# A graph kernel's first edge stretch: own rows in runs of four per partition

## The reference

```
src, dst = edges + one self loop per node
xl = x @ Wl ; xr = x @ Wr
logits = einsum(leaky_relu(xl[src] + xr[dst]), att)      # per edge and head
alpha  = softmax of the logits over the edges of one dst
out    = segment_sum(alpha * xl[src], dst) + bias        # then graph norm, elu, skip, layer norm
# twice: h = tanh(segment_sum(sum_b c[etype,b] * h[src] @ basis[b]) + h @ loop_w + bias)
```

## Time and profile before

| what | us |
|---|---|
| median of 3 runs | 3410.07 |
| lowest, highest | 3409.99, 3412.36 |
| profiled execution: its span, the only time the profile gives for it | 4033.8 |
| PE busy in the span | 3226.5 (80%) |
| POOL busy | 2055.6 (51%) |
| DVE busy | 2357.5 (58%) |
| ACT busy | 1828.3 (45%) |

### The profile page before, as it was taken

The page is one execution under the profiler, slowest core; times in us unless marked ns, Lnnn a source line. Parts: engine busy times, 40 slices in busy tenths (PEclk is TensorE's granted clock), DMA queues, the critical chain, the costliest instruction groups (busy, mean ns, idle before and its releaser), DMA issues.

```text
span 4033.8 us, 65767 instructions
## 1 busy us (share of the span) xinstructions
PE 3226.5 (80%) x17551; PEld 2290.4 (57%) x17551; DVE 2357.5 (58%) x7747; ACT 1828.3 (45%) x4347; POOL 2055.6 (51%) x2407
## 2 busy tenths in 40 slices
PE   3778777778778758888987888887996888886887
PEld 2666656666556545557874444445884444444665
DVE  3444344444444348897875666664444666665998
ACT  1333333334334324447993444443443444444665
POOL 5555555555555502225766666661226666662555
PEclk8988888889899879999998999998998988998999
DMA  3333333334333338877972333335993333333998
GB/s 82 97 101 95 93 93 92 94 95 105 92 94 102 86 78 239 241 230 252 291 253 81 88 84 83 83 83 167 299 299 88 84 82 81 84 85 117 341 326 279
DMA packets 660630, 579.29 MB, mean 144 GB/s; under 512 B 74468, under 2 KB 535173, under 8 KB 660261
## 3 DMA queue, kind: packets, MB, share of 16 engines
q1 hardware_dynamic: 494580, 335.02, 28.5%
q0 software_dynamic: 67008, 156.44, 14.3%
q10 hardware_dynamic: 98672, 83.61, 6.3%
HBM read 366.34 MB, written 208.43 MB: 142 GB/s over the span
## 4 chain that ended last, share of the span: by engine, by line
PE 36%; issue 16%; another core or an unknown queue 13%; ACT 12%; DVE 11%; DMA 4%; ACTq 3%; SPq 2%; POOL 1%; DVEq 0%; POOLq 0%
PE bank L1073 15%; PE bank L1084 4%; ACT work L1317 3%; PE bank L1120 3%; PE bank L1127 2%; DMA work<-w_d 2%; PE bank L1064 2%; DMA w_d<-work 1%; DVE work L1927 1%; ACTq L430 1%; ACT work L1309 1%; PE bank L1140 1%; PE bank L1094 1%; DVE work L1813 1%
## 5 line engine op out<-in xcount | busy, mean ns | idle before, releaser
L1927 DVE SCALAR_TENSOR_TENSOR work<-bank,coef,work 128x128 f32<-128x128 f32 x2400 | 664.5, 343 | 490.2 <-ACT work L1351 269.3
L1073 PE MATMUL bank<-basis_s,work 128*128 128x512 f32 x1600 | 815.9, 634 | 39.4 <-issue 18.1
L785 POOL DMA_INDIRECT work<-in_x_dram,slot_src x400 | 386.0, 965 | 497.5 <-PE bank L887 345.5
L827 POOL DMA_INDIRECT work<-h_d,slot_src x400 | 393.9, 985 | 230.2 <-issue 104.9
L827 POOL DMA_INDIRECT work<-x_d,slot_src x400 | 393.3, 983 | 226.9 <-issue 107.2
L785 POOL DMA_INDIRECT work<-in_x_dram,slot_dst x400 | 386.4, 966 | 123.6 <-issue 123.6
L1073 PEld LDWEIGHTS bank<-basis_s,work 128*128 128x128 f32 x1600 | 293.8, 205 | 272.9 <-issue 242.5
L1650 DVE TENSOR_TENSOR work<-work,bank 128x512 f32<-128x512 f32 x100 | 68.8, 688 | 608.5 <-ACT bank L1200 531.2
L1351 ACT ACTIVATE work<-bank,coef 128x128 f32<-128x128 f32 x800 | 288.4, 365 | 293.5 <-PE bank L1073 147.0
L1084 PEld LDWEIGHTS bank<-work 128*126 128x126 f32 x1600 | 217.9, 203 | 290.2 <-issue 228.3
L1084 PE MATMUL bank<-work 128*126 128x128 f32 x1600 | 233.3, 293 | 171.7 <-ACT work L1357 95.4
(11 more groups left out here) (278 smaller groups left out, 7547.7 us busy)
## 6 DMA issues: line engine op xcount, KB each, us to landing
w_d<-work SPq DMA_DIRECT2D x800, 62.5 KB
work<-in_x_dram SPq DMA_DIRECT2D x194, 256.0 KB, 4.5
work<-x_d SPq DMA_DIRECT2D x194, 256.0 KB, 4.4
w_d<-work SPq DMA_DIRECT2D x400, 66.9 KB
work<-w_d SPq DMA_DIRECT2D x398, 64.0 KB, 3.4
work<-w_d ACTq DMA_DIRECT2D x390, 64.0 KB, 3.4
xl_d<-work SPq DMA_DIRECT2D x97, 256.0 KB
work<-xl_d SPq DMA_DIRECT2D x97, 256.0 KB, 3.8
```

The lines of the kernel that those rows point to most:

```text
L785: pool.indirect_dma_start(quad(k, i % 3)[:, c, :], None, x, bass.IndirectOffsetOnAxis(ap=table[:, a:a + 1], axis=0)).then_inc(e_in[i % 3], 16)
L827: pool.indirect_dma_start(quad(0, i % 3)[:, c, :], None, (x1_d, h1_d)[l], bass.IndirectOffsetOnAxis(ap=slot_src[:, a:a + 1], axis=0)).then ...
L1073: pe.matmul(psum[YBANKS[k % 5]][:, :], quad(1, i % 2)[:, c, :], basis_s[:, l, :, :].rearrange("k b n -> k (b n)"), start=True, stop=True). ...
L1927: ins = dve.scalar_tensor_tensor(o, psum[YBANKS[k % 5]][:, b * D:(b + 1) * D], coef[:, i, l, c, b:b + 1], o, ALU.mult, ALU.add)
```

## The change

Loads and stores of the own rows go through `run_rows`. After the transposes, column t * 128 + p of bank A is then node 4p + t of the quad. ACT's copy writes it to column 4p + t, so that the copy in SBUF is in node order, as before; it now writes every element 16 bytes from the one before. The matmul for the self logits reads its stationary operand as before. The one for xl must leave node 4p + t in partition p of tile t, so that the store can go out in runs; its stationary operand is every fourth column, again 16 bytes apart. The last quad stays as it was.

```diff
             def load_own(q):
-                for to, part in node_quad(x, q, quad(9, q % 3), True):
+                for to, part in run_rows(x, q, quad(9, q % 3), True):
             def save_xl(q):
-                for to, part in node_quad(xl_d, q, quad(11, q % 3), False):
+                for to, part in run_rows(xl_d, q, quad(11, q % 3), False):
             def project_own(q):
+                runs = work[10][:, q % 2 * 512:(q % 2 + 1) * 512].rearrange("d (p t) -> d t p", t=4)
                 for t in range(4):
                     at = slice(t * P, (t + 1) * P)
-                    pe.matmul(LEFT[:, at], quad(10, q % 2)[:, t, :], w_lr[:, 0:D], start=True, stop=True)
+                    own = runs[:, t, :] if q < QUADS - 1 else quad(10, q % 2)[:, t, :]
+                    pe.matmul(LEFT[:, at], own, w_lr[:, 0:D], start=True, stop=True)
             def own_turned(q):
-                act.activation(flat(10, q % 2), A[:, :], ACT.Copy).then_inc(qt_cp, 1)
+                to, turned = quad(10, q % 2, P), A[:, :].rearrange("d (t p) -> d t p", t=4)
+                if q < QUADS - 1:
+                    to = flat(10, q % 2).rearrange("d (p t) -> d t p", t=4)
+                act.activation(to, turned, ACT.Copy).then_inc(qt_cp, 1)
```

## The result

The changed kernel takes 3455.36 us (median of 4 runs, 3454.96 to 3457.93) against 3410.03 us for the kernel before in the same session (3407.58 to 3412.36): 1.4% slower, ratio 1.0139 with a 95% interval of 1.0125 to 1.0153. The forecast was no change.

A forecast was written before the change was run, and what follows sets the result against it. The prediction took POOL's gathers to bound all three edge stretches, 10.0 us a row in the first, with PE close behind. Every term was 0 on the path, so 3410.07 + 0 = 3410 us, range 3385 to 3460.

The forecast's parts named there:

- weights of the xl matmul: Line 916, strided weight loads on PE: 0 to 0.88 us a row, taken as 0, covered by the matmul before.
- rival A: Line 916: strided weights make PE the bound, slower, 3422 to 3495 us, centre 3440; chance 0.24.
- POOL's pace as the bound before: First edge stretch: unprofiled, POOL's gathers set 10.0 us a row, inferred from 619.3 of 623.7 us profiled excess.
- The sign of being wrong at the prediction's end: Time moving over 7 us with POOL's spacing unchanged would mean the first stretch was not at POOL's rate.
- PE's need: First edge stretch: PE busy 9.68 of each 10.0 us row at full clock, 0.32 us to spare.
- The copy on ACT: Line 1184, strided write: 0 to 0.61 us more a row, covered, so value 0; without cover 59 us.
- Rival C: ACT's copy runs late and shows on PE's 926 and DVE's 1650: 3420 to 3439 us; chance 0.07.
- The transfers: Own rows' loads and stores in 2 KB pieces: 0.2 to 0.6 us less DMA time a row, off the path, 0.
- the trace disagrees: Against the DMA page's line rate from 512 bytes: 512 bytes took 28 ns, 2 KB 76 to 100.
- Rival B: Fewer pieces shorten late waits behind the two transfers, faster: 3352 to 3400 us, centre 3385; chance 0.26.

The follow-up runs named there:

- all_weights: The changed kernel with the self logits' matmul weights strided too, 16 strided loads a row in place of 8: 3555.0 us, ratio 1.041.
- weights_only: The kernel before with only the xl matmul's weights read at a 16-byte stride, for 97 quads: 3455.66 us, ratio 1.0118.
- half_weights: The changed kernel with only two of the four tiles' weights strided, four strided loads a row: 3408.71 us, ratio 0.9989.
- seven_before: The kernel before without the fourth chain's gather of destination rows from row 3 on, seven gathers a row: 3364.0 us, ratio 0.9848.
- runs_only: The kernel before with only the loads and stores of the own rows in runs of four: 3412.75 us, ratio 0.9989.
- before_again: The kernel before, unchanged, profiled a second time: ratio 1.0001, profiled span 3419.3 us.

## Why the prediction was wrong

**What failed.** The term "weights of the xl matmul": I took 0, the lower bound, on the ground that the load is covered by the matmul before it. It is not. PE spends 0.22 us on a float32 matmul without a stride and 0.465 with it; per load that is 0.12 us more, nearly all of the 320 - 191 = 129 ns by which the record grew. The price is 0.97 us a row from the timeline (0.95 between after and all_weights), above the upper bound of 0.88, and rival A's mechanism is what happened, by weights_only, all_weights and half_weights. The prediction's own words were a warning: a load is covered if it "stays under 0.11 us", and the record that it read took 208 ns. How much of a record is the engine's own time the trace of before does not tell.

**POOL's pace as the bound before: right, size off.** The inference from the excess of the first profile held in the main: in the second profile POOL waits for nobody, and the second stretch runs at 1.27 us a gather. That the sum closed to 4 us (619 of 624) was partly luck: the first stretch runs at 10.28 us a row, not 10.0, since some gathers take longer than their 944 ns median. So PE's room was 10.28 - 9.74 = 0.54 us a row, not 0.32. The sign of being wrong at the prediction's end misled too: the time moved by 45 us with the gathers as they were, and yet the first stretch had been at POOL's rate. What changed is that PE took over.

**PE's need: right in size, by luck.** 9.68 us a row was read, 9.74 measured with seven gathers. But 9.68 is the busy time of one row with pauses in it, and that row has no `weigh` (lines 960 and 965 do not run in it); rows with `weigh` need more. Where PE sets the pace, in seven_before, line 897 starts each row, and two rows without `weigh` lie between these:

```profile
509.93 1.13 PE L897 MATMUL bank<-work,w_lr 128*128 128x512 f32 x2
...
528.54 1.13 PE L897 MATMUL bank<-work,w_lr 128*128 128x512 f32 x2
```

That is 9.3 us for each, and 10.16 and 9.74 us for the rows with `weigh` around them (starts at 499.77 and 538.28). With the true numbers the sum closes: eight strided loads in 97 of the 99 intervals are 0.97 x 97 / 99 = 0.95 us, PE needs 9.74 + 0.95 = 10.69 us, POOL 10.28, so 0.41 us x 99 = 41 us of the stretch; measured 41.1 in the profiles, and 45 us (3455.36 - 3410.03) in the runs.

**The copy on ACT: right on cover, and the price was within the bounds.** 1107 to 1110 ns for 616 is +0.49 us a row (I had 0 to 0.61), with no effect alone (0.9999) or beside a second copy (1.0001). Rival C falls.

**The transfers: 0 on the path, right; their price, wrong.** The path is shown by runs_only. In all 660,629 - 586,133 = 74,496 packets are gone (74,500 foretold), but not the engines' time: the prediction had 0.2 to 0.6 us a row to gain, and runs_only shows none (28.1% and 28.4%). Its 100 ns a packet on q1 was a mean with small packets in it, about 1,500 of the 13,824 with four bytes; those of 2 KB alone took 112 ns there as well. Only on q10, in that other stage, were they faster, 85 ns. So "the trace disagrees" does not hold for the first stretch. Rival B falls; the waits that it was built on were not in the second profile.

**The chances.** A was given 0.24 with 3410 + 12 to 43 as its middle case, half the price; the result lay just past it, but by two errors that offset each other. The price was the full one and more (0.97), for which A's sum gives 3464 or more, and PE had 0.54 us of room, not 0.32. A rule on 16-byte lines, a full engine and eight instructions a row all pointed the same way. Against them stood only the cover, and the trace of before had no strided load to test it on.

## What to carry to other kernels

A repair of the order has to be paid on an engine that has room. Here PE and POOL were within 0.54 us of each other in a row of 10.28, and the same reordering is free on ACT and costs 45 us as strided weights on PE. And nearly half the packets of a queue fell away without any of its DMA time: before moving work to spare DMA, compare the packets' time and not their number, and ask which engine waits for nobody. Where loads and matmuls alternate without a pause, as here, count a slower load in full.

## What the runs showed of the hardware

- A float32 weight load of 128x128 takes 191 to 199 ns unstrided, 197 with elements 8 bytes apart, 320 with 16 bytes; in the stream of loads and matmuls the last means 0.465 us for two loads and two matmuls in place of 0.22.
- An ACT copy 128x512 from PSUM with the output 16 bytes apart takes 1104 to 1132 ns, against 616 to 618.
- In the first stretch a 2 KB packet of the own rows took 112 ns and one of 512 bytes 28 (runs_only, before_again): the same time for the same bytes.
- Gathers are not slowed by a fuller PE: with half the strided loads PE had no wait for gathered rows between 200 and 900 us and the gathers spanned 1028.3 - 17.5 = 1010.8 us, with none 1024.7. Why they are faster with more work on PE is open; the runs' times do not tell the two kernels apart (0.9989, 0.9977 to 1.0002).
- One profiled execution can be 18% longer than the same kernel unprofiled (4033.8 against 3410) and the next one not (3419.3). What its late waits were stays open; the times of the runs in the table leave no room for them.
